# A mixture-of-experts kernel on one core: narrow last tiles of experts laid over whole 128-column blocks, with one result transfer a block

## The reference

```python
def _L1_ffn_ref(x, router_w, w1, w2, w3):
    flat = x.reshape(-1, C)                                   # 8192 tokens, C = 64
    probs = softmax(flat @ router_w.T)                        # 8 experts
    topk_probs, topk_idx = jax.lax.top_k(probs, 2)
    topk_probs = topk_probs / (sum(topk_probs) + 1e-09)
    gates = einsum('nk,nke->ne', topk_probs, one_hot(topk_idx, 8))
    h1, h3 = einsum('nc,ehc->neh', flat, w1), einsum('nc,ehc->neh', flat, w3)   # H = 682
    y = einsum('neh,ech->nec', silu(h1) * h3, w2)
    return einsum('ne,nec->nc', gates, y)
t = t + _L1_ffn_ref(_ln_t(t), ...)
```

## Time and profile before

| what | value |
|---|---|
| runs timed | 970.32, 971.08, 974.22 us; median 971.08 |
| profiled execution, first to last instruction (span) | 969.5 us; the page gives no other time for that execution |
| mean granted clock of TensorE | 0.922 of full |
| busy of the span: TensorE, VectorE, ScalarE, GpSimd | 86%, 64%, 47%, 42% |
| L1243, the indirect transfers of results | 156, 153.2 us of GpSimd, 982 ns each |
| tiles of full width begin, narrow tiles end (TensorE) | about 570 us, 934.9 us |

### The profile page before, as it was taken

How to read it: one execution, slowest core, us unless ns; L and a number is a source line. 1 busy time by engine, 2 the same in 40 slices (tenths; PEclk the granted TensorE clock), 3 DMA queues, 4 the chain that set the end, 5 groups by cost and what they waited for, 6 DMA issues and landing times.

```text
span 969.5 us, 24022 instructions
## 1 busy us (share of the span) xinstructions
PE 829.5 (86%) x8420; PEld 505.2 (52%) x8420; DVE 623.7 (64%) x1425; ACT 456.7 (47%) x894; POOL 411.0 (42%) x524
## 2 busy tenths in 40 slices
PE   4775699999999788979998877869989999999940
PEld 4544477777777665647777752223323333333430
DVE  0452487878787466753887956768756666667644
ACT  2042466666666434444554534634535555555520
POOL 0000255555545311100245555666676774444570
PEclk9975799999999879998998889989989999999985
DMA  7115300000000199000000041052133332232108
GB/s 195 55 54 123 65 9 11 8 11 8 11 8 5 54 341 328 6 2 3 11 18 19 20 65 31 24 78 44 36 57 54 57 58 46 43 48 34 20 3 260
DMA packets 156254, 56.29 MB, mean 58 GB/s; under 512 B 121103, under 2 KB 150617, under 8 KB 156176
## 3 DMA queue, kind: packets, MB, share of 16 engines
q1 hardware_dynamic: 142736, 45.69, 20.9%
q0 software_dynamic: 9088, 8.55, 2.7%
q10 hardware_dynamic: 4352, 1.05, 0.5%
HBM read 25.09 MB, written 28.51 MB: 55 GB/s over the span
## 4 chain that ended last, share of the span: by engine, by line
PE 35%; DVE 10%; issue 4%; POOL 3%; DMA 2%; ACT 1%; SPq 1%; ACTq 0%; DVEq 0%; POOLq 0%
PE bank L1352 17%; PE bank L1362 9%; PE bank L1292 2%; POOL chosen_out L1243 2%; PE bank L1370 2%; POOL slot_x L1233 1%; PE bank L1283 1%; DVE norm_T L1751 1%; PE bank L1265 1%; PE bank L1274 1%; PE bank L1301 1%; DVE av_og L1501 1%; DMA slot_x<-rows,slots 1%; ACT norm_T L1459 1%; DVE residual L1771 1%
## 5 line engine op out<-in xcount | busy, mean ns | idle before, releaser
L1352 PE MATMUL bank<-ex_xt,ex_w 64*114 64x512 f32 (+7 forms) x936 | 216.6, 587 | 27.0 <-DVE ex_xt L1696 13.2
L1751 DVE TENSOR_TENSOR norm_T<-norm_T,bank 114x512 f32<-114x512 f32 (+7 forms) x234 | 142.0, 630 | 100.4 <-ACT norm_T L1459 98.5
L1243 POOL DMA_INDIRECT chosen_out<-ex_out,ex_id x156 | 153.2, 982 | 118.0 <-DVE norm_T L1751 42.0
L1459 ACT ACTIVATE norm_T<-bank 114x512 f32<-114x512 f32 (+7 forms) x234 | 129.9, 558 | 93.4 <-PE bank L1352 92.2
L1233 POOL DMA_INDIRECT slot_x<-rows,slots x128 | 125.3, 979 | 111.3 <-issue 64.4
L1352 PEld LDWEIGHTS bank<-ex_xt,ex_w 64*114 64x114 f32 x936 | 76.6, 178 | 142.7 <-issue 105.2
L462 POOL TENSOR_TENSOR probs<-shifted,win_rden 128x512 f32<-128x512 f32 x64 | 66.8, 1044 | 103.3 <-DVE win_rden L656 96.7
L1362 PE MATMUL bank<-norm_T,ex_w 114*64 114x512 f32 (+7 forms) x468 | 101.9, 571 | 0.3 <-ACT ex_w L1446 0.3
L642 DVE TENSOR_REDUCE win_max<-ps_s 128x8 f32<-128x512 f32 x64 | 43.9, 686 | 35.8 <-PE ps_s L502 35.8
L1362 PEld LDWEIGHTS bank<-norm_T,ex_w 114*64 114x64 f32 x468 | 30.1, 138 | 67.9 <-issue 49.8
L1452 ACT ACTIVATE norm_T<-bank 128x512 f32<-128x512 f32 (+7 forms) x39 | 21.8, 559 | 79.9 <-PE bank L1362 79.9
(11 more groups left out here) (259 smaller groups left out, 1482.9 us busy)
## 6 DMA issues: line engine op xcount, KB each, us to landing
slot_x<-blank SPq DMA_DIRECT2D x1, 17028.0 KB, 56.3
ex_x<-slot_x SPq DMA_DIRECT2D x128, 64.0 KB
norm_T<-chosen_out SPq DMA_DIRECT2D x8, 512.0 KB, 7.0
w_in<-in_L_ffn_w_dram SPq DMA_DIRECT2D x24, 168.0 KB
chosen_out<-ex_out,ex_id POOLq DMA_INDIRECT x156, 2.2
wlocal_in<-in_L_conv_w_local_dram SPq DMA_DIRECT2D x2, 1152.0 KB, 7.4
norm_T<-in_x_dram SPq DMA_DIRECT2D x4, 512.0 KB, 8.8
residual<-in_x_dram SPq DMA_DIRECT2D x4, 512.0 KB, 7.6
```

The lines of the kernel that those rows point to most:

```text
L1243: eng.indirect_dma_start(s.chosen_out[:, :], bass.IndirectOffsetOnAxis(ex_id[k % OUTS][0:depth(k), j:j + 1].bitcast(U32), 0), out[k % OUTS ...
L1352: eng.matmul(ps[b][0:HCHUNK, 0:width(k)], w13[par][halves(i), c * HCHUNK:(c + 1) * HCHUNK], xt[par][halves(i), 0:width(k)], start=True, st ...
L1459: eng.activation(act[c % DEEP][:, 0:width(k)], ps_1[c % DEEP][0:HCHUNK, 0:width(k)], ACT.Silu).then_inc(act_n, 1)
L1751: eng.tensor_tensor(h[par][:, c, 0:width(k)], act[c % DEEP][:, 0:width(k)], ps_3[c % deep3(k)][0:HCHUNK, 0:width(k)], ALU.mult).then_inc(h ...
```

## The change

The seven narrow tiles are cut into blocks of 128 rows, the last one shorter, where they were cut into four equal quarters. `blocks(k)` is 4, 3, 3, 2, 2, 1, 1 for the tiles 32 to 38 (16 in all; before it was 28), `rows_of(k, j)` is 128, or 64 in the last block of tiles 32, 34, 36 and 38. `turn_out` makes one transposition a block, `result` works on 128 partitions and `blocks(k)` columns of gates, `scatter` starts one transfer a block, and `all_added` waits for the smaller count. The load of the gates and numbers now reads all 512 rows of the slot in each tile. The 32 wide tiles, the four band loads and the widths of the matrix products stay as they are. The order of the work on each engine stays too; instructions are dropped or change their shape.

```diff
--- before.py
+++ after.py
@@ -1129,13 +1129,17 @@
             for k in range(EARLY + OUTS * ROUNDS, FTILES):
                 body(k, k % OUTS, k // OUTS)
 
-        def depth(k):
-
-            return P if sym(k) or k < 2 * TOK // SLOT else P - (k + 1 - 2 * TOK // SLOT) * P // EXPERTS
-
         def width(k):
 
-            return R * depth(k)
+            return SLOT if sym(k) or k < 2 * TOK // SLOT else SLOT - (k + 1 - 2 * TOK // SLOT) * SLOT // EXPERTS
+
+        def blocks(k):
+
+            return -(-width(k) // P)
+
+        def rows_of(k, j):
+
+            return min(P, width(k) - j * P)
 
         def not_first(k):
             return sym(k) or k > 0
@@ -1154,7 +1158,7 @@
 
         def all_added(eng):
             for i, landed in enumerate(added):
-                eng.wait_ge(landed, adds(len(range(i, FTILES, len(added)))))
+                eng.wait_ge(landed, 16 * sum(blocks(k) for k in range(i, FTILES, len(added))))
 
         def store(eng, q, j):
             eng.dma_start(out_rows[j][:, part(q), :], s.x1[j * BATCH:(j + 1) * BATCH, part(q), :]).then_inc(stored, 16)
@@ -1184,7 +1188,7 @@
                         lane = band % 2 * B32
                         eng.dma_start(x[k % 4][band * B32:(band + 1) * B32, 0:width(k)].rearrange("t (b c) -> t b c", c=B32),
                                       src[:, :, lane:lane + B32].rearrange("o (b t) c -> (o t) b c", t=B32)).then_inc(x_in[k % 4], 16)
-                    eng.dma_start(gate_id[k % 4][0:depth(k), :, :], src[:, :, C:C + 2].rearrange("o (r p) c -> (o p) r c", p=depth(k)),
+                    eng.dma_start(gate_id[k % 4][:, :, :], slot_x[bass.ds(tile, 1), :, C:C + 2].rearrange("o (r p) c -> (o p) r c", p=P),
                                   allow_slow_non_contiguous=True).then_inc(x_in[k % 4], 16)
                 eng.wait_ge(oc_n, FTILES)
                 all_added(eng)
@@ -1237,11 +1241,12 @@
 
                 def scatter(k):
                     eng.wait_ge(oc_n, k + 1)
-                    for j in range(R):
+                    for j in range(blocks(k)):
                         if j > 0 and k + 2 < FTILES:
                             eng.wait_ge(h_n, HCHUNKS * (k + 2) + j + 1)
-                        eng.indirect_dma_start(s.chosen_out[:, :], bass.IndirectOffsetOnAxis(ex_id[k % OUTS][0:depth(k), j:j + 1].bitcast(U32), 0),
-                                               out[k % OUTS][0:depth(k), j, :], None, bounds_check=2 * TOK - 1, oob_is_err=False).then_inc(added[k % OUTS], 16)
+                        some = slice(0, rows_of(k, j))
+                        eng.indirect_dma_start(s.chosen_out[:, :], bass.IndirectOffsetOnAxis(ex_id[k % OUTS][some, j:j + 1].bitcast(U32), 0),
+                                               out[k % OUTS][some, j, :], None, bounds_check=2 * TOK - 1, oob_is_err=False).then_inc(added[k % OUTS], 16)
 
                 eng.wait_ge(s.blank_n, 16)
                 send(0, 0, PAIR, 1)
@@ -1366,8 +1371,8 @@
                 def turn_out(k):
                     eng.wait_ge(yc_n, k + 1)
                     wait(eng, both_n, k)
-                    for r in range(R):
-                        last = eng.transpose(ps_t[0:depth(k), r * P:(r + 1) * P], y[:, r * depth(k):(r + 1) * depth(k)], s.ident[:, :])
+                    for r in range(blocks(k)):
+                        last = eng.transpose(ps_t[0:rows_of(k, r), r * P:(r + 1) * P], y[:, r * P:r * P + rows_of(k, r)], s.ident[:, :])
                     last.then_inc(eo_n, 1)
 
                 def body(k, ring, eights):
@@ -1687,8 +1692,8 @@
                     if sym(k) or k >= OUTS:
                         eng.wait_ge(added[ring], adds(eights))
                     eng.wait_ge(x_in[buf], 16 * LOADS * (quarter + 1))
-                    eng.tensor_copy(ex_gate[ring][0:depth(k), :], gate_id[buf][0:depth(k), :, 0])
-                    eng.tensor_copy(ex_id[ring][0:depth(k), :], gate_id[buf][0:depth(k), :, 1]).then_inc(gate_n, 1)
+                    eng.tensor_copy(ex_gate[ring][:, :], gate_id[buf][:, :, 0])
+                    eng.tensor_copy(ex_id[ring][:, :], gate_id[buf][:, :, 1]).then_inc(gate_n, 1)
 
                 def turn_in(k, par, buf, quarter):
                     eng.wait_ge(x_in[buf], 16 * LOADS * (quarter + 1))
@@ -1698,10 +1703,11 @@
                 def result(k, ring):
                     eng.wait_ge(eo_n, k + 1)
                     wait(eng, oc_n, k)
-                    eng.tensor_reduce(both[0:depth(k), :, :], ps_t[0:depth(k), :].rearrange("p (r i c) -> p r c i", i=2, c=C), AX.X, ALU.add).then_inc(both_n, 1)
+                    n = blocks(k)
+                    eng.tensor_reduce(both[:, 0:n, :], ps_t[:, 0:n * P].rearrange("p (r i c) -> p r c i", i=2, c=C), AX.X, ALU.add).then_inc(both_n, 1)
                     eng.wait_ge(both_n, k + 1)
-                    eng.tensor_tensor(out[ring][0:depth(k), :, :], both[0:depth(k), :, :],
-                                      ex_gate[ring][0:depth(k), :].unsqueeze(2).to_broadcast([depth(k), R, C]), ALU.mult).then_inc(oc_n, 1)
+                    eng.tensor_tensor(out[ring][:, 0:n, :], both[:, 0:n, :],
+                                      ex_gate[ring][:, 0:n].unsqueeze(2).to_broadcast([P, n, C]), ALU.mult).then_inc(oc_n, 1)
 
                 def routing_beside(k, c):
                     if (k, c) == (0, 1):
```

## The result

The changed kernel took 961.27 us (median of 4 runs, 958.76 to 962.99) against 971.25 us of the kernel before in the same runs; the ratio is 0.989, 95% interval 0.986 to 0.992. Timed again in a later comparison it was 0.991, 0.988 to 0.994. The forecast was 961.2 us.

The account below looks back on a forecast made before the run. GpSimd's queue of transfers after the narrow tiles was taken to hold up the whole core for 10 us. 0 (wide tiles) - 10.1 + 0.2 = -9.9 us, from 971.08 to 961.2 us; range 958.8 to 964.0, 8 times in 10.

Parts of the forecast that it names:

- Step 1: GpSimd's scatters, 28 to 16: twelve fewer at 1.14 to 1.28 us, 13.7 to 15.4 us of queue, not all on the path.
- Step 2: VectorE's results on one block, 0.28 and 0.22 us: about 0.60 us saved for each of tiles 37 and 38, earlier savings hidden.
- Step 3: TensorE's transpositions, 28 to 16: 0.33 us saved behind tile 38; of the other nine, 0.3 taken between bounds 0 and 1.3.
- Steps 4 and 5: Starts of the single transfers of tiles 37 and 38: 934.56 and about 935.8 in place of 945.90, a gain of 10.1 us.
- Step 6: Larger gate loads in tiles 32 to 38: costed at nothing, 2.5 us of landing against 11.5 us of lead in tile 38.
- Step 7: Final loads, sums and stores after the last landing: 21.7 us, unchanged, only starting sooner.
- The sum: Whole kernel: 0 for wide tiles, - 10.1 + 0.2 = -9.9 us, taking 971.08 to 961.2 us.
- Cost by the row: Rival, chance 0.04: GpSimd's time follows rows, so only 0.9 us of results and transpositions could show; 970.2 to 971 us.
- slower by late gates: Rival, chance 0.02: tile 38's full gate load lands 26 us after issue and holds up VectorE's transposition; 976 us.
- More comes through: Rival, chance 0.08: TensorE's nine inner transpositions are all on the path; gain 10.9 us, 960.2 us, perhaps 959.
- Dearer transfers: Rival, chance 0.06: each of the last four transfers costs 0.4 us more, landing 1 us more; gain some 7.3, 963.8 us.
- transfers above 1.2 us: Sign that the forecast is wrong: GpSimd transfers taking longer than 1.2 us.

Follow-up runs that it names:

- number put back: Changed kernel with each narrow tile again starting four transfers, the twelve added ones of 16 rows into scratch tensors; 972.83 us, ratio 1.000 to the kernel before.
- both four: Changed kernel with four transpositions and results over all four blocks in each narrow tile, transfers as changed; 962.07 us in one run.

## Why the prediction was right, step by step

- **What bounds the kernel** was read rightly: a queue of transfers that ran on for 10 us after everything else. The number put back took the whole gain back.
- **Step 1, the pitch.** 1.14 to 1.28 us a transfer; measured in added ones 1.14 to 1.17 (9.27 us for eight, 3.55 for three). The twelve were priced at 13.7 to 15.4 us of queue, with 10.1 of it on the path; measured, 9.95 for the change and 10.07 (35.20 - 25.13) for putting them back.
- **Step 2, results.** Forecast 0.28 and 0.22 us for one block, measured 0.28 to 0.29 and 0.22 to 0.23; 0.60 us on the path, measured 0.61. That the earlier tiles' shorter results stay hidden holds too: made long again they moved VectorE's last chunk by 0.01 us.
- **Step 3, transpositions.** The last one takes 0.30 where 0.27 was read from the rows; of the inner nine 0.3 was taken to come through. From the first transfer of tile 32 to VectorE's last chunk were 933.37 - 910.82 = 22.55 us, now 932.21 - 909.83 = 22.38: 0.17, where the run with the transpositions put back has 0.26. So the 0.3 was up to 0.13 us too much, and the true value nearer still to the lower bound. The chain goes through ScalarE's copy of w2, as rows 9 suggested.
- **Steps 4 and 5, the last two starts.** Forecast 934.56 and 935.8 on the old time line; measured 933.67 and 934.96, which is 934.66 and 935.95 when moved by the 0.99 us by which this execution was ahead. The queue, and not tile 38's data, decides the last one, as was said, by 0.13 us. The landing is 0.09 us longer, where 0.2 was taken.
- **Step 6, gates** costed at nothing: nothing at four times the load.
- **Step 7, the last part**: 21.69 us from the landing to the end before, 21.64 now.
- **The sum** was 9.9 us and is 9.91. That it fits to a hundredth is luck: the last start gained 9.95 us and not 10.1, the landing cost 0.09 and not 0.2, and the last part gave 0.05 that no step had. The lower bound of the forecast's own range is also slightly off: with nothing passing through step 3 and a landing of 2.2 us, the steps give 945.90 - 936.14 - 0.29 = 9.5 us of gain and not 9.6. That the span fell by 10.9 was the start of the narrow tiles, which no step had, and which differs between executions by up to 4 us; the forecast made the span's gain and the median's one number. The medians (971.25 and 961.27) differ by 9.98 us, in runs that spread over 4 us on either side, and the later comparison, with the same G, has 973.7 and 964.05, 9.65 apart. So the mechanism and its 9.9 us are borne out by G; that the median came within 0.1 us of the forecast is luck.
- **The rivals.** Cost by the row and slower by late gates fall to runs. "More comes through" needed 1.3 us of the inner transpositions on the path and got 0.17 to 0.26. "Dearer transfers" had a real mechanism, shown below, but none of the last four met it; those of the narrow tiles take 1.01 us at most. The sign "transfers above 1.2 us" could tell nothing if taken over all tiles: the longest, in the wide ones, is 1.336 us now and was 1.331 before.

The Trainium skill's price for a transfer issued by GpSimd (page "DMA: Bandwidth & Descriptors", section "Anatomy of one DMA", 2.0 us fixed, mostly receipt) is seen here in the landing of 2.0 us, which is paid once at the end. What the removed transfers gave back is GpSimd's own 1.15 us each, which that split calls small; here the measurement decides.

## What to carry to other kernels

Look at which queue is still at work when the engines are done, and count its instructions: an indirect transfer costs its issuing engine by the piece (here 1.14 us for 16 rows, 1.28 for 128), so work that shrinks by rows should shrink by number of transfers. Once such a queue runs dry between results, the order on the engines behind it decides, and pieces taken out pay only in part: here twelve that were worth 13.7 to 15.4 us of queue gave 9.95 with all that went with them. To see parts of a microsecond in a kernel whose executions differ by 4 us, measure in the trace from an event that the edit cannot move.

## What the runs showed of the hardware

- **A transfer that starts inside VectorE's copy of w13 takes longer.** In the run with the number put back:

```profile
924.95 0.52 DVE L1693 TENSOR_SCALAR ex_w<-w 128x684 f32 x1 [0.42 <-issue]
```

The transfer that starts at 925.07 took 1.27 us where its neighbours take 0.98: 0.29 more, with 0.40 us of the copy still to go. With both four it was 1.25 us at 927.72, the copy from 927.59 on, and with the longer results alone 1.25 us at 927.38; before the change 1.11 in place of 0.91, 0.32 us of overlap. In the wide tiles of the changed kernel it recurs, and there the longest of all its transfers is one that starts 0.04 us into a copy, the first two rows here:

```profile
761.80 0.51 DVE L1687 TENSOR_SCALAR ex_w<-w 128x684 f32 x1
761.84 1.34 POOL L1248 DMA_INDIRECT chosen_out<-ex_out,ex_id  x1 [0.30 <-issue]
...
768.55 0.43 DVE L1709 TENSOR_TENSOR ex_out<-ex_both_halves,ex_gate 128x256 f32<-128x256 f32 x1
768.63 1.20 POOL L1248 DMA_INDIRECT chosen_out<-ex_out,ex_id  x1 [0.30 <-issue]
```

Another, 0.35 us into a copy, at 868.69, takes 1.01. These transfers of 128 rows (1.34, 1.27, 1.25 and 1.01 us) all end 0.85 to 0.87 us after the end of the copy, however early in it they began, so what one loses is bounded by what is left of the copy. The last two rows show that it is not the copy alone: the multiplication by the gates, with both inputs in SBUF, lengthens a transfer in the same way (768.98 to 769.83 is 0.85 again). In the other order the copy can be the longer one: the one at 902.90, begun 0.53 us into a transfer, took 0.79 us in place of 0.51; but the one at 921.94, begun 0.20 us into a transfer, took 0.52 and the transfer 0.98, so an overlap alone is not enough. The page "SBUF — State Buffer" of the Trainium skill, section "Who interferes with whom", says that where the two need the ports that VectorE and GpSimd share, the one that issues first keeps them for its whole instruction and the other waits. The transfers that come second agree with that; the copies agree only in part. The extra time of about 2.5 us that the same page gives for a transfer beside a `tensor_copy`, in its section "A bandwidth-pool intuition that's wrong", never occurs here: the most is 0.36. That a transfer of 16 rows meets the copy as readily as one of 64 or 128 was not tried.

- **The granted clock can fall within the last microsecond of work, or just after it**, in kernels with the same work: at 933 to 934 us in the run with smaller gate loads, during the last product; during the last transposition in the run with four times the gate loads; and after TensorE was done in the changed kernel (done at 933.45, the window from 935 to 936 us has 0.95). It cost tile 38's result 0.30 and 0.11 us, and the path 0.15 and nothing.
